# The order of four key lengths in the attention and scan stage of a decoder layer

## The reference

```python
x = x + attention(layernorm(x))            # 16 query heads, 2 key/value heads, head width 32, causal
x = x + selective_scan(ctx, layernorm(x))  # 16 states for each of 512 channels, scan over 512 steps
x = x + experts(layernorm(x))              # 16 experts, top 2 of them, and a shared expert
```

## Time and profile before

| | |
|---|---|
| Time, median of 3 runs | 1238.64 us (1237.73 to 1240.28) |
| Time of the profiled execution | 1238.74 us |
| Its span in the profile | 1236.9 us |
| Mean granted TensorE clock | 0.974 of full speed |
| Busy share of the span | PE 87%, DVE 65%, ACT 54%, POOL 54% |
| First and last `top` of `mix` | 171.3 and 686.3 us from the span's start |

### The profile page before, as it was taken

The page is one execution under the profiler, slowest core; times in us unless marked ns, Lnnn a source line. Parts: engine busy times, 40 slices in busy tenths (PEclk is TensorE's granted clock), DMA queues, the critical chain, the costliest instruction groups (busy, mean ns, idle before and its releaser), DMA issues. The chain is left out here.

```text
span 1236.9 us, 18614 instructions
## 1 busy us (share of the span) xinstructions
PE 1073.2 (87%) x6368; PEld 642.0 (52%) x6368; DVE 806.6 (65%) x1195; ACT 668.3 (54%) x1438; POOL 673.2 (54%) x587
## 2 busy tenths in 40 slices
PE   7999838888888888888888899999999989999970
PEld 3444325555555555555555444444444457676740
DVE  5477779999999999999999476631760013333327
ACT  3566768889888888898888424202010012223220
POOL 1033369999999999999999630202041124444430
PEclk9999959999999999999999999999999999999995
DMA  6210001101111111111331212103027314333219
GB/s 204 87 36 19 18 18 35 35 28 35 35 36 32 30 35 36 36 33 63 95 102 45 90 48 103 69 34 116 20 79 244 102 44 128 127 128 129 77 49 385
DMA packets 51820, 94.74 MB, mean 77 GB/s; under 512 B 9806, under 2 KB 17998, under 8 KB 51728
## 3 DMA queue, kind: packets, MB, share of 16 engines
q1 hardware_dynamic: 44208, 72.82, 17.9%
q0 software_dynamic: 7520, 20.72, 5.4%
HBM read 74.51 MB, written 20.84 MB: 77 GB/s over the span
## 5 line engine op out<-in xcount | busy, mean ns | idle before, releaser
L604 POOL TENSOR_TENSOR w_all<-w_all 128x512 f32<-128x512 f32 x256 | 321.1, 1275 | 0.6 <-POOLq L96 0.3
L778 DVE TENSOR_TENSOR_SCAN w_all<-da,w_all 128x512 f32<-128x512 f32 x256 | 298.0, 1206 | 0.0
L712 ACT ACTIVATE da<-w_all,a_flat 128x512 f32<-128x512 f32 x256 | 179.6, 702 | 9.0 <-PEq L96 7.7
L683 PE MATMUL yb<-ident,w_all 128*128 128x128 f32 x1024 | 161.6, 281 | 7.5 <-DVE acc L786 7.5
L633 PE MATMUL sc<-w_all,attn 32*128 32x384 f32 (+3 forms) x512 | 105.0, 486 | 45.5 <-ACT w_all L720 22.8
L720 ACT ACTIVATE w_all<-sc,neg_max 128x128 f32<-128x128 f32 (+3 forms) x256 | 134.1, 539 | 16.5 <-DVE neg_max L770 15.5
L659 PE MATMUL ob<-w_all,v 128*32 128x128 f32 x1280 | 94.7, 277 | 52.8 <-ACT w_all L729 52.8
L683 PEld LDWEIGHTS yb<-ident,w_all 128*128 128x128 f32 x1024 | 113.5, 141 | 37.0 <-issue 30.6
L770 DVE TENSOR_REDUCE neg_max<-sc 128x2 f32<-128x256 f32 (+3 forms) x128 | 104.2, 814 | 34.2 <-PE sc L636 34.2
L1166 POOL TENSOR_TENSOR w_all<-w_all 128x512 f32<-128x512 f32 x24 | 29.4, 1226 | 165.0 <-ACT w_all L1337 165.0
L729 ACT ACTIVATE w_all<-tb 128x256 f32<-128x256 f32 (+2 forms) x192 | 102.8, 535 | 29.7 <-PE tb L648 29.7
(11 more groups left out here) (199 smaller groups left out, 1630.6 us busy)
## 6 DMA issues: line engine op xcount, KB each, us to landing
w_all<-b_scratch SPq DMA_DIRECT2D x64, 256.0 KB, 3.3
w_all<-in_w_up SPq DMA_DIRECT2D x16, 512.0 KB, 6.0
w_all<-in_w_down SPq DMA_DIRECT2D x16, 512.0 KB, 6.8
w_all<-sorted_y SPq DMA_DIRECT2D x16, 512.0 KB, 10.3
attn<-in_x SPq DMA_DIRECT2D x4, 1024.0 KB, 6.8
w_all<-in_x SPq DMA_DIRECT2D x16, 256.0 KB, 4.1
norms<-attn SPq DMA_DIRECT2D x4, 1024.0 KB, 4.3
out_dram<-acc SPq DMA_DIRECT2D x16, 256.0 KB, 8.9
```

What stands on the lines that cost most here:

```text
L604: pool.tensor_tensor(dbu[:, k, :], keep["du"][i // N][:, k * T:(k + 1) * T], b_all[i % 2][:, :], ALU.mult).then_inc(pool_dbu.sem, pool_dbu ...
L683: last = pe.transpose(yb[which][:, k * P:(k + 1) * P], state[i % 2][:, k, t * P:(t + 1) * P], ident[:, :])
L712: act.activation(da[unit % 2][:, :], keep["dt"][i // N][:, k * T:(k + 1) * T], ACT.Exp, scale=keep["a_flat"][:, unit % (N * KD):unit % (N ...
L778: dve.tensor_tensor_scan(state[i % 2][:, k, :], da[unit % 2][:, :], dbu[:, k, :], 0.0, ALU.mult, ALU.add).then_inc(dve_scan.sem, dve_scan. ...
```

## The change

A tuple `LENGTHS` gives the query block of each of the four places in a group. Before, place 0 to 3 held lengths 1, 2, 3, 4; after, they hold 1, 4, 2, 3. Whether a unit is split is asked of its length and no longer of its place, so that split units stand at c1 and c3 in place of c2 and c3. All else follows: the same instructions with the same shapes are issued, and the loop, the buffers, the waits and the work of the scan stay as they are.

```diff
+LENGTHS = (0, 3, 1, 2)
...
         def place(unit):
-            p, j = unit // NT, unit % NT
+            p, j = unit // NT, LENGTHS[unit % NT]
             quad, half = p // 2, p % 2
             return quad // NT, quad % NT, half, j
+
+        def split(unit):
+            return LENGTHS[unit % NT] >= 2
...
-                for part in range(1 if (g - 2) % NT < 2 else 2):
+                for part in range(2 if split(g - 2) else 1):
                     turn[g - 2, part] = len(turn)
 
         def last_turn(unit):
-            return turn[unit, 0 if unit % NT < 2 else 1] if unit >= 0 else -1
+            return turn[unit, 1 if split(unit) else 0] if unit >= 0 else -1
 
         def heads_of(unit, part):
-            return (0, 1) if unit % NT < 2 else (part,)
+            return (part,) if split(unit) else (0, 1)
...
             def turn_prob(unit, part):
-                j = unit % NT
+                j = LENGTHS[unit % NT]
...
-                if 0 <= g - 2 < UNITS and (g - 2) % NT >= 2:
+                if 0 <= g - 2 < UNITS and split(g - 2):
                     turn_prob(g - 2, 1)
...
             def turned(unit, part):
-                n = (unit % NT + 1) * P
+                n = (LENGTHS[unit % NT] + 1) * P
...
-                    if (g - 2) % NT >= 2:
+                    if split(g - 2):
                         turned(g - 2, 1)
...
             def top(unit):
-                n = (unit % NT + 1) * P
+                n = (LENGTHS[unit % NT] + 1) * P
```

## The result

The changed kernel takes 1264.64 us (median of 4 runs, 1261.07 to 1265.45) against 1239.24 for the kernel before (4 runs, 1237.73 to 1240.28). The ratio is 1.0201, with a 95% interval of 1.0183 to 1.0218: 25 us slower, where 13.6 were forecast. The profiled execution took 1265.45 us with a span of 1263.6, 26.7 us more than the span before.

A forecast was written before the change was run, and what follows sets the result against it. No engine was taken as full; waits between engines set the quad's length. Four legs summed to 33.43 us a quad against 32.58, +13.6 us over 16 quads on 1238.74: 1252.3 us, range 1244 to 1260.

The forecast's parts named there:

- the legs: Stretches of a quad between `top` of c1 and of c3: c3 to c1 8.27 us, c1 to c3 7.93, or 8.86 with the spread.
- the term for the clock: TensorE's clock in steady quads: stays at 1.00, adding nothing; as a rival, falls to its lower level, at most 1492 us, chance 0.02.
- the ends: First steps, where the pipeline fills, and last three, where it drains: set at zero with 1.5 us to either side.
- +0.85 a quad: Steady quad of eight steps: 33.43 us against 32.58, over 16 quads +13.6 us.
- No change, because the fullest engine has the same work: DVE's work in a quad is untouched and its waiting only moves: time stays 1238.7 us, chance 0.05.
- Faster, because long scores get a step to themselves: PE begins `weigh_v` 4 earlier, c3-c1 legs fall to DVE's own 6.98 us: -29 us, 1209, chance 0.07.

The follow-up runs named there:

- both edits together: ACT's second copy put ahead of `weigh_c` and four more transposes in each of c1 and c3, against the changed kernel: 1248.97 us, ratio 1.0068.

## Why the prediction was wrong

Its direction and the mechanism of the legs held, its size didn't: 1252.3 was forecast with a range to 1260, and 1264.64 came. The step that failed is the term for the clock, which the sum had at nothing; the ends, also at nothing, add less.

- *The legs.* Each of the four came within 0.04 us, and their sum, 33.43, within 0.01 of the quads at full clock. This is the term "+0.85 a quad". The run with transposes in c0 (+0.86) and the one with the copy moved (-0.75) show that the chain runs where the prediction put it: through ACT's second copy, and through PE's work in c0 to the scores of length 4. The quads confirm it directly: the forecast took 16 of them at +0.85, and 15 of them have it.
- *The clock: the step that failed.* The prediction treated a fall of the clock as all or nothing, priced it at 240 us and gave it 0.02, because PE's longest pause "stays near 1 us as it is now", and it counted on a granted clock that stays. What came is in between: the clock falls for 3.42 us in 7 of 15 quads, 1.5 us each, 10.7 in all. PE's busy share at full clock, 27.32 / 33.42 = 82%, is what was forecast. The longest pause hardly grew either: 1.02 us, and before 0.99:

```profile
428.42 0.49 PE L633 MATMUL sc<-w_all,attn 32*128 32x128 f32 x4 [0.99 <-ACT w_all L720]
```

What grew is how many stand together: 0.89 and 0.69 in c1 and c2, up to 0.52 and 1.02 in c3 and c0, where before the 0.99 of c3 had 0.23 behind it and the 0.70 and 0.69 of c1 and c2 stood further apart (417.53 and 422.04, 4.5 us; now 452.18 and 454.12, 1.9 us). That the clock falls behind such pairs is shown by the runs that filled them. With both filled, three runs had the clock at 1.00 in all 15 quads; with one filled alone, 6 or 7 long quads stayed in each of three runs, and every fall lay behind the pair left open. The Trainium skill, "TensorE: Matmul & The Clock Gate", section "A second HAM failure mode: psum-queue depth-cycling", says that frequent short pauses make the clock go back and forth. The trace of the changed kernel agrees, with 0.50 for 3.42 us at a time; the trace of before, at 1.00 with pauses of 0.99, had been taken to speak against it.
- *The ends.* They were set at zero with 1.5 us to either side. The first quad came out 4.3 us longer. With the pauses filled its length is 31.65 to 31.76, so some 2.9 of the 4.3 come with the clock: its mean in the first quad is 0.72 in the changed kernel, 0.82 to 0.83 with the pauses filled and 0.86 in the kernel before. How the other 1.4 us divide between legs and clock isn't shown. Behind the last reciprocal 1.4 us are gained. Together the parts give the profiled execution: 1252.3 - 0.9 (15 quads in place of 16) + 10.7 + 4.3 + 0.4 - 1.4 = 1265.4 us.
- *The rivals.* "No change, because the fullest engine has the same work" fell: DVE's busy time in a quad is 30.10 as before, and the quad is longer all the same. "Faster, because long scores get a step to themselves" fell with the waits of 1.12 and 1.34 us before length 4; the order 1, 2, 4, 3 gets faster with the two long lengths side by side: its scores of length 3 come beside the longest maxima, and its second copies stay behind short exponents, as before. No run takes these two apart.

What stays open: why the clock fell in about every second quad here and in 12 of 15 in the run with the copy moved, why behind the same pair of pauses it fell in one half of a quad and not in the other, why transposes added in c0 brought more falls with the pauses unchanged, and whether the new pause of 0.95 us is what gives the order 2, 3, 4, 1, with quads only 0.03 us longer than before, its six falls. The runs show which pauses a fall follows; they don't give a bound that would have told it ahead.

## What to carry to other kernels

In a software pipeline with single buffers, cut the period at the starts of one instruction and add up the chain from one to the next, engine by engine; this gave the periods of six kernels within 0.3 us (this change, the transposes in c0, the copy moved, the two other orders, and both edits together), and showed which order is worth trying. Then ask separately whether TensorE keeps its clock, and price a partial loss too: a change that costs a little on the chain may cost nearly as much again in clock, here 10.7 us beside 12.7. Neither the busy time nor the longest pause told the cases apart: in a quad the kernel before has 27.47 of 32.58 us and a pause of 0.99 and kept its clock, and the order 2, 3, 4, 1 has 27.44 of 32.61 us and a pause of 0.99 and lost it in 6 of 15 quads. Look for quads of unequal length first; equal work in unequal time at a lower granted clock tells the two apart.

## What the runs showed of the hardware

- TensorE's granted clock went to 0.50 for 3.42 us at a time in 7 of 15 quads of the changed kernel, with pauses of 0.89 and 0.69 us just in front and none above 1.02 us in the quad, though the engine was busy for 27.32 of 33.42 us at full clock. Each fall made its quad 1.5 to 1.6 us longer.
- The falls followed the pauses that were left open: in c2 in the changed kernel and with c3 filled, in c0 with c1 filled, none with both filled.
- Work added to TensorE in both pairs of pauses kept the clock up, whether transposes or products (quads of 33.6 us at 1.00 in both). Transposes added where it is the late engine brought more stretches of low clock (two in ten of 15 quads of the profiled execution).
- The order 1, 2, 4, 3 is 1.4% faster than the kernel before (ratio 0.9864, 0.9848 to 0.9881), with the same instructions.
